# Two transfers of 1024 columns in place of one of 2048 for each high transpose

## What is computed

```python
h = jnp.maximum(_layernorm(x), 0.0)
ht = (h @ W).reshape(N, 4, 256).transpose(1, 0, 2)
src, dst = einsum("hnd,hd->hn", ht, a_src), einsum("hnd,hd->hn", ht, a_dst)
e = leaky_relu(src[:, :, None] + dst[:, None, :], 0.01) + adj[None]
x = x + einsum("hij,hjd->hid", softmax(e), ht).mean(axis=0)

h = jnp.maximum(_layernorm(x), 0.0)
A = (adj != 0)
x = x + A @ (h @ W1 + b1) / A.sum(axis=0)[:, None]
```

## Time and profile before

| | |
|---|---|
| median of three runs | 593.96 us |
| lowest, highest | 588.38, 595.82 us |
| the profiled execution | 591.1 us, span 589.3 us |
| mean granted TensorE clock in it | 0.962 of full speed |
| high products, first and last start | 85.7 and 516.3 us |

### The profile page before, as it was taken

One profiled execution on the slowest core, in us unless ns is written; L12 is line 12 of the kernel. 1 busy time (PEld: TensorE's weight loads), 2 busy tenths in 40 slices (PEclk: granted clock), 3 DMA queues, 4 the chain that ended last, 5 costly groups with the idle time before them and its releaser, 6 DMA issues.

```text
span 589.3 us, 8989 instructions
## 1 busy us (share of the span) xinstructions
PE 527.6 (90%) x2992; PEld 308.1 (52%) x2992; DVE 455.2 (77%) x586; ACT 453.9 (77%) x379; POOL 31.5 (5%) x64
## 2 busy tenths in 40 slices
PE   6998889997988989797989798979989899878996
PEld 6843335453645545454555454535545455556885
DVE  6567868897969697787888798969887796637984
ACT  3477968998879797979799799878997987254860
POOL 3100000000000000000000000000000000001221
PEclk7799999998989899999999899989998999999999
DMA  8029428999999999999999999999999999961111
GB/s 307 7 73 304 94 50 152 229 204 222 210 196 237 198 229 190 221 182 233 208 225 204 227 209 213 222 211 234 200 232 202 229 204 214 196 225 63 40 41 45
DMA packets 300263, 108.76 MB, mean 185 GB/s; under 512 B 284720, under 2 KB 295360, under 8 KB 297680
## 3 DMA queue, kind: packets, MB, share of 16 engines
q1 hardware_dynamic: 300208, 108.45, 85.8%
q10 hardware_dynamic: 32, 0.01, 0.0%
HBM read 30.81 MB, written 6.32 MB: 63 GB/s over the span
## 4 chain that ended last, share of the span: by engine, by line
SPq 40%; PE 27%; DMA 10%; issue 9%; DVE 7%; ACT 7%; POOLq 0%; DVEq 0%; ACTq 0%
SPq L305 17%; SPq L313 14%; PE ps_q L796 9%; PE ps_relu L861 8%; DMA probs_hi_t<-probs_hi 7%; PE ps_q L805 3%; SPq L323 3%; ACT logits L548 2%; ACT ps_relu L540 2%; PE ps_q L772 2%; SPq L275 1%; SPq L297 1%; DVE logits L1015 1%; DVE probs_lo L1024 1%; ACT probs_hi L556 1%
## 5 line engine op out<-in xcount | busy, mean ns | idle before, releaser
L796 PE MATMUL ps_q<-h_w_split,probs_hi_t 128*128 128x512 f16 x1024 | 254.7, 394 | 40.9 <-DMA probs_hi_t<-probs_hi 39.3
L796 PEld LDWEIGHTS ps_q<-h_w_split,probs_hi_t 128*128 128x128 f16 x1024 | 95.8, 100 | 161.0 <-issue 39.1
L540 ACT ACTIVATE ps_relu<-dst_rows,src_bias 128x2048 f32<-128x2048 f32 x63 | 124.0, 1969 | 59.0 <-DVE small L1015 58.6
L1015 DVE CUSTOM_DVE_ANT_0 logits<-ps_relu,adj_rows 128x2048 f32<-128x2048 f32 x48 | 110.0, 2291 | 53.1 <-PE ps_relu L782 50.9
L805 PE MATMUL ps_q<-h_w_split,probs_lo_t 128*128 128x256 f16 x1024 | 122.3, 273 | 0.7 <-DMA probs_lo_t<-probs_lo 0.7
L1024 DVE SCALAR_TENSOR_TENSOR probs_lo<-logits,small,probs_hi 128x2048 f16<-128x2048 f32 x48 | 112.7, 2348 | 4.8 <-ACT probs_hi L556 4.8
L805 PEld LDWEIGHTS ps_q<-h_w_split,probs_lo_t 128*128 128x128 f16 x1024 | 100.0, 98 | 24.8 <-DMA probs_lo_t<-probs_lo 1.5
L548 ACT ACTIVATE logits<-logits,small 128x2048 f32<-128x2048 f32 x48 | 95.5, 1989 | 0.0
L556 ACT ACTIVATE probs_hi<-logits,small 128x2048 f16<-128x2048 f32 x48 | 95.4, 1988 | 0.0
L861 PE MATMUL ps_relu<-hidden_split,mask_columns 128*128 128x512 f32 x256 | 60.0, 393 | 2.8 <-DVE hidden_split L1109 1.5
L861 PEld LDWEIGHTS ps_relu<-hidden_split,mask_columns 128*128 128x128 f32 x256 | 47.8, 188 | 13.6 <-DVE hidden_split L1109 2.2
(11 more groups left out here) (89 smaller groups left out, 320.4 us busy)
## 6 DMA issues: line engine op xcount, KB each, us to landing
adj_rows<-in_adj SPq DMA_DIRECT2D x16, 1024.0 KB, 6.5
dst_rows<-dst_scratch SPq DMA_DIRECT2D x4, 1024.0 KB, 5.5
x_all<-in_x SPq DMA_DIRECT2D x4, 512.0 KB, 6.8
x<-in_x SPq DMA_DIRECT2D x16, 128.0 KB, 2.5
x_scratch<-x SPq DMA_DIRECT2D x16, 128.0 KB, 1.9
hidden_scratch<-hidden SPq DMA_DIRECT2D x16, 128.0 KB, 2.3
out<-out_rows SPq DMA_DIRECT2D x16, 128.0 KB, 1.7
x_in<-x_scratch SPq DMA_DIRECT2D x1, 1792.0 KB, 10.0
```

The source lines that it names most:

```text
L540: nc.scalar.activation(R[:, :], rows, ACT.Relu, scale=(1.0 - SLOPE) / SLOPE, bias=src[:, bass.ds(u, 1)]).then_inc(relu_ready, 1)
L796: last = nc.tensor.matmul(ACC[parity][:, :], TA[:, e, b, :], H[:, h, b, :], start=(h == 0 and b == 0), stop=False)
L1015: nc.vector.tensor_tensor_reduce(out=logits_of(h, parity), in0=R[:, :], in1=ADJ[:, parity, :], scale=-1.0, scalar=3.0e38, op0=ALU.add, op1 ...
```

## The change

The transpose of `PA` is issued as two transfers, of the first and of the second 1024 columns. The first adds to `hi_in`, the second to the new semaphore `hi_late_in`. PE waits for the first ahead of the first high product, and for the second ahead of the ninth, behind the seed. ACT's `high` and the first casts of the aggregation, which waited for the one landing, wait for both.

```diff
             def transpose_hi(u, e):
                 sp.wait_ge(probs_hi_ready, u + 1)
                 passed(u)
                 if past(u, 2):
                     sp.wait_ge(hi_multiplied, u - 1)
                     passed(u)
-                sp.dma_start_transpose(TA[:, e, :, :], PA[:, e, :]).then_inc(hi_in[e], 16)
+                for half, landed in ((0, hi_in), (1, hi_late_in)):
+                    b = slice(CH * half, CH * (half + 1))
+                    sp.dma_start_transpose(TA[:, e, b, :], PA[:, e, CH * P * half:CH * P * (half + 1)])\
+                        .then_inc(landed[e], 16)
...
                 act.wait_ge(rinv_ready, v + 1)
                 if past(v, 2):
                     act.wait_ge(hi_in[h % 2], 16 * k)
+                    act.wait_ge(hi_late_in[h % 2], 16 * k)
...
                     for e in range(2):
-                        act.wait_ge((hi_in, lo_in)[q][e], 16 * UNITS // 2)
+                        act.wait_ge((hi_late_in, lo_in)[q][e], 16 * UNITS // 2)
+                        act.wait_ge(hi_in[e], 16 * UNITS // 2)
...
                     if b == NB // 2 and has(u + 4):
                         seed(u + 4, h)
+                    if b == NB // 2:
+                        pe.wait_ge(hi_late_in[e], 16 * (k + 1))
                     last = nc.tensor.matmul(ACC[parity][:, :], TA[:, e, b, :], H[:, h, b, :],
                                             start=(h == 0 and b == 0), stop=False)
```

More of the change, by code:

```diff
@@ L202, in gnn_kernel @@
         hi_in = [sem("hi_in0"), sem("hi_in1")]
+        hi_late_in = [sem("hi_late_in0"), sem("hi_late_in1")]
         lo_in = [sem("lo_in0"), sem("lo_in1")]
```

## The result

The changed kernel took 601.66 us as the median of four runs (600.59 to 601.86), beside 594.08 for the kernel before (four runs). The ratio is 1.016, with a 95% interval of 1.012 to 1.020: slower beyond its interval, but inside the 2% that the prediction calls "within". That is 9.5 us by the ratio and 7.6 us between the medians, where +9 was forecast and 603 us named. The profiled execution took 600.59 us, 9.5 more than the 591.1 of before, at a mean granted TensorE clock of 0.955 (0.962 before).

The account below looks back on a forecast made before the run. The DMA engines pace most of a block, with holes where SyncE's lead runs out. Place terms sum to 0.78 us a block, +8 over ten loop blocks, +1 for straight-line blocks: 594 + 9 = 603 us, range 590 to 620.

Parts of the forecast that it names:

- The time of a half: SyncE's queue: a half issue holds it 1.24 us, a pair 2.53; first halves land about 3.2 us after issue.
- A whole transpose's floor of 1.33: SyncE's queue: a full transpose holds it at least 1.33 us; time above that is waiting for the DMA engines.
- The stores, +0.34: High of h=1, then two stores, then low: a hole of 0.25 exists, so 0.34 us less lead adds in full, per block.
- The x load, +0.10: High of h=3, then x load, then low: 2.21 us needed, 2.11 covered after the split, so +0.10 us a block.
- Head 2 (+0.29): High transpose behind the loop's edge or the mask, lead already gone: second half and following low add 0.29 us a block.
- head 0 (+0.05): High transpose behind the adjacency load: the load's data hide the pair; 0.05 us a block allowed for scatter.
- Nothing carries over.: Each low transpose gives SyncE its full lead back, its 2.44 us of data exceeding its 1.33 us floor.
- The straight-line blocks, +1: Four blocks outside the loop, also paced by SyncE, with shorter gaps: 0.3 us each allowed, +1 us together.
- The early start at 0: PE's first eight high products may start 1.2 us sooner; worth 0 in the middle, 22 us if on the path.
- Hidden: Rival, chance 0.20: second issue overlaps the first's data wholly, or a half's floor is under 1.0 us; 594 us, give or take 3.
- SyncE becomes the bound: Rival, chance 0.23: halves take the mask transpose's median of 1.42 us in SyncE's queue; 627 us, or 612 to 627 partly hidden.
- Faster: Rival, chance 0.07: PE's transpose waits are on the path through `hi_multiplied`, saving 1.2 us at each of 18 waits; 572 us.

Follow-up runs that it names:

- quarters: Changed kernel with four transfers of 512 columns per high transpose, PE waiting for each ahead of its four products: 717.35 us, ratio 1.218 to the kernel before.
- the four alone: Four kernels, each the changed kernel with only one head's high transpose per block split (heads 0, 1, 2, 3): ratios to the kernel before 0.998, 1.010, 1.002, 0.998.

## Why the prediction was right, point by point

- **What bounds it.** Right, and now shown: from 200 to 475 us SyncE waits for 0.2 us in the kernel before and for nothing in the changed one, and 0.34 us of idle time behind each high transpose costs nearly as much as the change. What the profile alone didn't tell is how near the next bound lies. With whole transposes, moving the stores and giving them to GpSimd both ran into DVE's `probs_lo` at once, with 8.5 and 8.9 us of waits.
- **The time of a half.** Right in size: floor 1.23 for the 1.24 taken, and a second half, which follows with no wait between, holds the queue 1.33 as the median. The pair alone is 2.61 us (344.29), not 2.53. The first halves land 3.56 us after their issue as the median, not 3.2.
- **A whole transpose's floor of 1.33.** Misread. The shortest whole ones are exceptions in the kernel before; 1.94 is what the lone one took, and 1.76 to 1.9 what they take in the kernel with quarters. It did not hurt this sum, which went by the lead at the end of an issue, but it did hurt the forecast for the quarters.
- **The stores, +0.34.** Mis-sized: 0.17 and 0.18 in the changed kernel's two profiles, 0.16 at its place alone. The sum let the first store take its time whatever stands ahead. In truth that issue is elastic too: it held the queue 0.69 us behind a whole transpose and 0.40 behind a pair (means of seven blocks), and so gave 0.29 of the 0.34 back.
- **The x load, +0.10.** Mis-sized: 0.34 and 0.28 in the changed kernel, 0.28 at its place alone. The step that failed is that lead and x data cover the way to the low issue behind a pair. The low there landed 4.44 us after its issue in the kernel before and 4.52 in the changed one, hardly more than the 4.25 of the lone transpose at 62.72, which speaks for a low that was already late. But only some 0.2 of the growth stands ahead of that low's landing; the rest, 0.16 and 0.06 in the two profiles, stands at the mask behind it, for which the sum had no term. And 0.34 us of idle time in the same place lengthened it by 0.02 only, as a spare of 0.24 would let one expect. So why a pair costs more there than its shorter lead is not settled.
- **Head 2 (+0.29) and head 0 (+0.05).** 0.27 and 0.00 in the changed kernel, 0.36 and -0.28 in its second profile.
- **"Nothing carries over."** Not borne out: with one head split, places that are not split change by up to 0.33 us, be it by the split or by the code around it. That is at least a part of why the four alone make half of the whole.
- **The straight-line blocks, +1.** Misread. SyncE was to wait for ACT only before about 128 us. These are its waits in the kernel before from 128 to 200 us (total us, times, longest):

```profile
SPq L305 <- ACT probs_hi L556: 15.1, 4, 4.4
SPq L313 <- DVE probs_lo L1024: 4.4, 3, 1.7
```

So the compute engines paced part of each of these blocks. The term itself stays unproven: from the adjacency load at 98.60 to that at 213.22 the changed kernel took 3.1 us more than the kernel before, and in its second profile 1.0 more. The DMA row, too, stands at 9 from slice 8 to 35, not from 9 to 33; nothing hangs on that.
- **The sum.** 0.78 a block forecast; 0.79 by the landings and 0.84 by the loads in one profile, 0.54 and 0.78 in the other (nine blocks for the loads). Right to the hundredth is luck: two terms erred by -0.24 and +0.17, and the sum by landings moves by 0.25 from profile to profile. That 603 us came within 1.4 of the measured time also rests on the base of 594; measured later, the kernel before took 588.66 to 590.53.
- **The early start at 0.** Right within some 8 us, of 22 at stake. Forecast wrong in a detail: PE's longest wait was to be a microsecond shorter. It is 3.26 us behind the adjacency load in the block shown, where it was 3.08:

```profile
334.83 3.60 PE L804 MATMUL ps_q<-h_w_split,probs_hi_t 128*128 128x512 f16 x8 [3.26 <-DMA probs_hi_t<-probs_hi]
```

- **The rivals.** "Hidden" holds for head 0 only. "SyncE becomes the bound" did not come at halves; it came at quarters. "Faster" would have needed SyncE to wait in the loop, and there it did not.

No version tried beats the kernel before beyond its interval; the nearest are the two with head 0 or head 3 alone split, at 0.998.

## What to carry to other kernels

Before you split a transfer, look at who waits: where the issuing queue never waits and its consumers do, an earlier first half is worth nothing and the second issue is charged to the path. Charge it by where the split stands in the queue, not by the mean: behind the long adjacency load it cost nothing here, ahead of the short x load most. Take a second profile before you trust a growth of 0.3 us in one place, and expect the places beside it to move too. And before you relieve such a queue, look for the engine it will meet next.

## What the runs showed of the hardware

The time for which a DMA transpose of 128 partitions holds SyncE's queue hardly depends on its size below 1024 two-byte columns: 1.27 us as the median at 512 columns, 1.33 at 1024, and 1.76 to 1.94 at 2048 (the lone one, and the low ones beside the quarters), though a few of these took 1.33. The 16 DMA engines moved a lone whole one at 209 GB/s; by that rate, as an estimate, the data of 512 columns (0.131 MB) take 0.63 us, half as long as their issue. Transfers of 128 KB issued by GpSimd landed 1.5 to 2.6 us later after their issue than the same ones issued by SyncE.
